# Two tiles at a time in the routed layers of a small fused transformer, with two smaller reorderings

## The reference, cut to what matters

```python
# layers 0 and 1, feed-forward: the best 2 of 8 experts for each token
logits = xn @ gate_w
top_logits, top_idx = jax.lax.top_k(logits, TOP_K)
h = jax.nn.gelu(jnp.einsum('td,edh->teh', xn, w1) + b1, approximate=False)   # 192 -> 768
y = jnp.einsum('teh,ehd->ted', h, w2) + b2                                   # 768 -> 192
# layer 2, attention: a local and a linear attention, mixed by a learned gate
# (sigmoid of a small network), then an output product
# layer 2, feed-forward: 8 sub-spaces of 16 features, the best 4 of 64 small experts in each
z = jnp.einsum('nd,sdr->nsr', xf, P)
scores = jnp.einsum('nsr,smr->nsm', z, C)
topv, topi = jax.lax.top_k(scores, K)
```

## Time and profile before

| what | value |
|---|---|
| median of 3 runs | 2105.56 us (2104.97 to 2110.13) |
| the profiled execution | 2113.81 us, of which the span of the trace is 2112.1 us |
| PE busy in the span | 1833.6 us, 87% |
| routed layers, tiles | about 291 to 451 us and 697 to 852 us of the span |
| fusion and gates | about 1031 to 1312 us |
| sub-experts | about 1313 to 1660 us |

### The profile page before, as it was taken

How to read it: one execution, slowest core, us unless ns; L and a number is a source line. 1 busy time by engine, 2 the same in 40 slices (tenths; PEclk the granted TensorE clock), 3 DMA queues, 4 the chain that set the end, 5 groups by cost and what they waited for, 6 DMA issues and landing times. The chain is left out here.

```text
span 2112.1 us, 38740 instructions
## 1 busy us (share of the span) xinstructions
PE 1833.6 (87%) x13908; PEld 1330.6 (63%) x14000; DVE 1218.9 (58%) x3641; ACT 837.8 (40%) x1667; POOL 379.5 (18%) x380
## 2 busy tenths in 40 slices
PE   5989969987885999788898775899999899979997
PEld 3678759966664799577655442333333588657886
DVE  1478842237998222488535544788888567792221
ACT  1145413324551111245335545667667355311111
POOL 1100112133311331431001101000000000123543
PEclk8999979998995899899898877999999999999999
DMA  5000345520004554102000104900000000304662
GB/s 200 1 1 0 115 136 179 187 57 18 12 0 142 168 187 156 30 19 85 0 1 17 48 29 128 291 24 1 1 1 1 24 1 0 133 13 132 188 179 64
DMA packets 83839, 156.75 MB, mean 74 GB/s; under 512 B 22390, under 2 KB 57942, under 8 KB 82806
## 3 DMA queue, kind: packets, MB, share of 16 engines
q1 hardware_dynamic: 63669, 134.71, 19.6%
q0 software_dynamic: 19552, 19.63, 3.9%
q10 hardware_dynamic: 480, 0.63, 0.1%
HBM read 125.04 MB, written 29.48 MB: 73 GB/s over the span
## 5 line engine op out<-in xcount | busy, mean ns | idle before, releaser
L2375 DVE TENSOR_TENSOR l2s_gated<-l2s_hidden,ps 128x408 f32<-128x408 f32 x512 | 262.8, 574 | 58.9 <-PE ps L2280 58.5
L2345 ACT ACTIVATE l2s_hidden<-ps,pack_l2f 128x816 f32<-128x816 f32 x256 | 227.0, 938 | 98.7 <-PE ps L2272 98.0
L129 PE MATMUL ps<-pack_const 128*128 128x512 bf16 x496 | 147.4, 432 | 40.6 <-PEq L163 13.7
L2280 PE MATMUL ps<-l2s_gs,l2s_spread 96*128 96x408 bf16 x512 | 150.5, 340 | 0.3 <-DVE l2s_gated L2375 0.3
L2272 PE MATMUL ps<-l2s_zs,l2s_up 128*128 128x408 bf16 x512 | 132.7, 341 | 15.7 <-DMA l2s_down<-in_sub_down 15.7
L1895 PE MATMUL ps<-l_down,l_hidden 128*128 x792 | 139.8, 326 | 0.0
L1895 PEld LDWEIGHTS ps<-l_down,l_hidden 128*128 128x128 f32 x792 | 127.3, 190 | 0.4
L129 PEld LDWEIGHTS ps<-pack_const 128*128 128x128 bf16 x588 | 59.4, 108 | 100.5 <-issue 62.4
L2290 PE MATMUL ps<-l2s_gated,l2s_down 128*32 128x408 f32 x1024 | 114.3, 518 | 4.0 <-DVE l2s_comb L2362 3.8
L2272 PEld LDWEIGHTS ps<-l2s_zs,l2s_up 128*128 128x128 bf16 x512 | 39.6, 97 | 120.5 <-ACT l2s_hidden L2345 82.2
L1854 POOL DMA_INDIRECT l_xt<-rows_in,l_tokens x66 | 63.1, 956 | 255.3 <-PE ps L1867 196.1
(11 more groups left out here) (468 smaller groups left out, 4007.4 us busy)
## 6 DMA issues: line engine op xcount, KB each, us to landing
l_up<-in_l_up SPq DMA_DIRECT2D x66, 576.0 KB, 3.8
l3c_wg<-in_l_gate SPq DMA_DIRECT2D x16, 576.0 KB, 4.9
l3c_wu<-in_l_up SPq DMA_DIRECT2D x16, 576.0 KB, 6.2
l3c_wd<-in_l_down SPq DMA_DIRECT2D x16, 576.0 KB, 3.9
slots_out<-l_y SPq DMA_DIRECT2D x66, 96.0 KB, 2.4
l_down<-in_l_down SPq DMA_DIRECT2D x8, 675.0 KB, 9.5
g_parts<-l2b_g_parts SPq DMA_DIRECT2D x12, 408.0 KB, 4.4
l_down<-in_l_down SPq DMA_DIRECT2D x8, 576.0 KB, 7.5
```

The lines of the kernel that those rows point to most:

```text
L129: pe.matmul(bank, halves[:, 0:128], halves[:, :], start=True, stop=True)
L2280: pe.matmul(gate_bank(n), spread[:, t % 8, :], gs[half][2 * r + odd][:, t // 8, pair, chunk(n % 2), :], start=True, stop=True).then_inc(ga ...
L2345: act.activation(hidden[:, p % kept, :, :], ps[:, 0, 2 * (p % 2):2 * (p % 2) + 2, 0:NG], ACT.Gelu_apprx_tanh, bias=w.at("b1")[:, s * MT + ...
L2375: dve.tensor_tensor(gated[:, n % ring, :], hidden[:, n // 2 % kept, n % 2, :], gate_bank(n), ALU.mult)\
```

## The change

Three things are changed.

1. Routed layers, on PE and DVE: tiles go in pairs. For tiles i and i + 1 PE makes the whole-row products of both, then the half-row products of both, then the transposes of tiles i + 2 and i + 3, then the second products of tiles i - 2 and i - 1. DVE follows the same order. `hidden` gets four buffers instead of two. The program of SP and that of POOL stay as they are.
2. Fusion and gates: on PE `lin_outputs(q)`, on DVE `lin_results(q)` and `fuse(q - 1)` now stand ahead of `step(at[2])` instead of behind it. ACT stays.
3. Sub-experts: the two parts of a block of weights have a semaphore each; the first product waits for the first part alone, the second product for the second part. SP issues the first part ahead of the block's gate parts.

```diff
-                step(at[2])
                 if q < G:
                     lin_outputs(q)
+                step(at[2])
...
-                step(at[2])
                 if q < G:
                     lin_results(q)
                 if 1 <= q <= G:
                     fuse(q - 1)
+                step(at[2])
                 step(at[3])
...
-        hidden = m.sb("hidden", [128, 2, FM, 128])
+        hidden = m.sb("hidden", [128, 4, FM, 128])
...
             transposes(0)
-            for i in range(TILES):
-                up_products(i)
-                if i + 1 < TILES:
-                    transposes(i + 1)
+            transposes(1)
+            for i in range(0, TILES, 2):
+                two = range(i, min(i + 2, TILES))
+                for n in two:
+                    whole_products(n)
+                for n in two:
+                    half_row_products(n)
+                for n in two:
+                    if n + 2 < TILES:
+                        transposes(n + 2)
                 if i:
-                    down_products(i - 1, expert_of(pe, i - 1))
-            down_products(TILES - 1, expert_of(pe, TILES - 1))
+                    for n in (i - 2, i - 1):
+                        down_products(n, expert_of(pe, n))
+            for n in two:
+                down_products(n, expert_of(pe, n))
...
-                if i >= 2:
-                    act.wait_ge(y_ps, i - 1)
+                if i >= 4:
+                    act.wait_ge(y_ps, i - 3)
...
             rows_turned(0)
+            rows_turned(1)
-            for i in range(TILES):
-                if i + 1 < TILES:
-                    rows_turned(i + 1)
+            for i in range(0, TILES, 2):
+                two = range(i, min(i + 2, TILES))
+                for n in two:
+                    if n + 2 < TILES:
+                        rows_turned(n + 2)
                 if i:
-                    result(i - 1)
-            result(TILES - 1)
+                    for n in (i - 2, i - 1):
+                        result(n)
+            for n in two:
+                result(n)
...
-                        pe.wait_ge(weights_loaded[k], 32)
+                        pe.wait_ge(up_loaded[k], 16)
...
+                    if not half and t == 0 and pair == 0 and at % 2 == 0:
+                        pe.wait_ge(down_loaded[2 * r + odd], 16)
```

More of the change, by code:

```diff
@@ L1868, in transposes, with whole_products @@
                 last.then_inc(xtT_ps, 1)
-            def up_products(i):
+            def whole_products(i):
                 pe.wait_ge(xtT_ready, i + 1)
@@ L1879, in up_products, with half_row_products @@
                                   xtT[:, i % 2, 0, :], start=(t == 0), stop=False, skip_group_check=True)
+            def half_row_products(i):
                 for t in range(3):
@@ L1894, in down_products @@
                 for t in range(FM):
-                    last = pe.matmul(y_bank(i), hidden[:, i % 2, t, :], wd[:, t * D:(t + 1) * D],
+                    last = pe.matmul(y_bank(i), hidden[:, i % 4, t, :], wd[:, t * D:(t + 1) * D],
                                      start=(t == 0), stop=(t == FM - 1))
@@ L1973, in _ @@
                             n = 3 * half + t
-                            last = act.activation(hidden[:, i % 2, n, :], hid_bank(i, half)[:, t * 128:(t + 1) * 128],
+                            last = act.activation(hidden[:, i % 4, n, :], hid_bank(i, half)[:, t * 128:(t + 1) * 128],
                                                   func, bias=b1[:, n:n + 1])
                     else:
-                        last = act.activation(hidden[:, i % 2, 3 * half:3 * half + 3, :].rearrange("p t n -> p (t n)"),
+                        last = act.activation(hidden[:, i % 4, 3 * half:3 * half + 3, :].rearrange("p t n -> p (t n)"),
                                               hid_bank(i, half), func)
@@ L2198, in sub_experts @@
         comb_ps, comb_ready, comb_added = m.sem("comb_ps"), m.sem("comb_ready"), m.sem("comb_added")
-        weights_loaded = [m.sem(f"weights_loaded{k}") for k in range(4)]
+        up_loaded, down_loaded = ([m.sem(f"{name}_loaded{k}") for k in range(4)] for name in ("up", "down"))
         parts_loaded = [[m.sem(f"parts_loaded{half}{k}") for k in range(4)] for half in range(2)]
@@ L2230, in _, with up_weights, down_weights @@
         def _(sp):
-            def weights(k):
+            def up_weights(k):
                 first = 4 * (k // 2) + k % 2
                 sp.dma_start(up_parts[k][:, :, :], g["up_pairs"][first:first + 3:2, :, :].rearrange("s k n -> k s n"))\
-                  .then_inc(weights_loaded[k], 16)
+                  .then_inc(up_loaded[k], 16)
+            def down_weights(k):
+                first = 4 * (k // 2) + k % 2
                 sp.dma_start(down[k][:, :, :, :].rearrange("p s t r -> p s (t r)"),
                              dram["sub_down"].rearrange("p (s n) -> p s n", s=NS)[:, first:first + 3:2, :])\
-                  .then_inc(weights_loaded[k], 16)
+                  .then_inc(down_loaded[k], 16)
             def parts(half, k):
@@ L2244, in parts @@
                   .then_inc(parts_loaded[half][k], 16)
-                if half or k:
-                    gate_parts(sp, half, k)
             sp.dma_start(spread_raw, dram["sub_spread"]).then_inc(spread_loaded, 16)
@@ L2252, in _ @@
                     if not half:
-                        weights(k)
+                        up_weights(k)
+                    if half or k:
+                        gate_parts(sp, half, k)
+                    if not half:
+                        down_weights(k)
                     if not half and k == 2:
```

## The result

The changed kernel takes 2194.34 us in the median (2190.86 to 2198.7) against 2107.85 us for the kernel before in the same series: ratio 1.0401, 95% interval 1.0371 to 1.0431. That is 86 us slower, where 60 were forecast; 2194 lies in the range given (2125 to 2202), near its upper end.

The account below looks back on a forecast made before the run. PE was taken to bound most stages, a chain through PE, ACT and DVE the fusion. Pairing -11, pauses +62, clock +22, fusion -12, sub-experts -1 give +60 on 2105.6: 2166 us, range 2125 to 2202.

Parts of the forecast that it names:

- The pauses: Routed layers: PE waits 2.2 us for weights ahead of odd tiles 5 to 31, 28 times, 62 us.
- The chain: Routed layers, after second products end at E: store E + 0.59, load E + 1.72, weights landed E + 5.5.
- rival 2: Routed layers: every pause costs clock, 2188 us, or loads also land half a microsecond later, 2202; chance 0.12.
- The clock: Routed layers: every second pause brings a stretch at half clock, 14 x 1.6 = 22 us lost.
- Rival 1: Routed layers: the clock holds through the pauses, 2144 us; chance 0.18.
- What pairing saves: Routed layers: 0.34 us for going into half-row products and out, paid once per two tiles, saves 11 us.
- The fusion: Fusion: the three PE pauses before the fused transposes go, 12 us saved, bounds 0 and 16.
- The sub-experts: Sub-experts: the first product no longer waits for the second part of the weights, 1 us saved, between 0 and 3.
- The sum: Whole kernel: -11 + 62 + 22 - 12 - 1 = +60 us, giving 2166 us for the median.
- the forecast's own range: Whole kernel: 2145 to 2190 us around the predicted 2166, with chance 0.50.
- rival 3: Routed layers: the pauses don't come, the store doesn't hold up the load or slack hides it; 2082 us; chance 0.13.

## Why the prediction was right, and where its sizes were off

**The pauses** came where they were forecast, ahead of each odd tile from 5 to 31, for the reason forecast: the load stands behind a store, and the store's result was moved behind the transposes. Moving the load was enough to undo them. The term was mis-sized: 62 us forecast, 75.5 measured, 2.7 us each instead of 2.2. The chain went the same way, most links a little longer. The second products end at 372.76 + 12 x 0.163 = 374.71; the store is issued at +0.72 (forecast 0.59), the load at +1.80 (1.72), and PE starts again at +5.92 (5.5), that is 4.1 us after the load's issue instead of 3.8. The loads now land more slowly, which the old median could not show:

```profile
DMA to landing us min/median/max: 3.5/4.5/7.5
```

against 3.8 before. That figure mixes both kinds: from tile 5 on the odd tiles' loads land in 4.1 us in the median, the even ones, which go out while the odd one is still under way, in 4.8. Only the odd ones' 0.3 us counts for the pauses. This was named under rival 2, with half a microsecond. The forecast's other figure, 3.35 us by the Trainium skill ("DMA: Bandwidth & Descriptors", section "Anatomy of one DMA"), is an estimate from a fit that the page gives for DMAs issued by GpSimd, and SP issues these; it was too low here.

**The clock.** 22 us forecast for every second pause, 31.1 measured. The step that was mis-sized is the share of pauses, which was a guess between none and all: one of two was taken, and the trace's record of the granted clock has a stretch at 0.50 behind 19 of the 28, 11 in layer 0 and 8 in layer 1. Each lasts 3.4 us and so costs 1.7, which makes 32 us. Rival 1, the clock that holds, is out: idle times of 2.1 to 3.2 us, once in 11 to 14 us, were enough to lose the full clock again and again, while others of 1.8 to 2.8 us went by without it. The Trainium skill ("TensorE: Matmul & The Clock Gate", section "HAM oscillation") has only longer idle gaps as harmful; the measurement decides. The length of the pause alone doesn't tell which outcome comes. Behind the pause of 2.46 us shown above the clock stayed at 1.00, behind the next one, of 2.45 us, it was 0.50:

```profile
392.04 2.07 PE L1878 MATMUL ps<-l_xtT,l_up 128*128 128x128 f32 x12 [2.45 <-issue]
393.00:396.40 3.40, 3.40 (x28) 3.17 (x28) 0.00 (x0) 0.51 (x2) 0.00 (x0) 0.50 0.06 26
```

What a slow stretch costs is seen on the half-row products of two pairs in succession, 2.86 us at the low level and 1.54 at the high one:

```profile
369.25:372.11 2.86, 2.86 (x25) 2.64 (x24) 0.00 (x0) 1.01 (x4) 0.00 (x0) 0.50 0.00 2
382.14:383.68 1.54, 1.54 (x25) 1.42 (x25) 0.00 (x0) 0.40 (x2) 0.00 (x0) 1.00 0.15 56
```

**What pairing saves**: 11 us forecast, 11.9 measured with the pauses gone. In the steady part two tiles took 9.05 us and a pair takes 8.71, the forecast's 0.34; the rest lies in the layers' starts.

**The fusion**: 12 us forecast, 13.4 in the profile, which alone is good to some 5 us, and 14 (8 to 18) in the timed runs of that part alone. For q = 2 the forecast had DVE's scores of the next step 11.5 us after the end of `gates`. In the changed kernel `gates` end at 1212.95 and the scores start here:

```profile
1211.94 1.01 DVE L1535 TENSOR_TENSOR rows_z<-ps,pack_l2a 102x384 f32<-102x384 f32 x2
1217.27 0.86 PE L1243 MATMUL ps<-pack_const,rows_z 102*96 102x102 f32 x8
1222.26 0.89 ACT L1392 ACTIVATE pack_l0f<-ps 96x408 f32<-96x408 f32 x2
1223.89 1.11 DVE L1579 MAX8 l2b_best<-x 102x8 f32<-102x64 f32 x8 [1.51 <-ACT x L1414]
```

That is 10.9 us, against 15.4 before. PE's transposes are early, at 1217.27, and their results lie until ACT copies them at 1222.26, behind its part of the step, as forecast. A little of the wait moved from L1243, where 11.6 us are gone, to L1305, which waited 5.5 us for ACT before and waits 7.4 now, three times each.

**The sub-experts**: 1 forecast, 1.0 in the profile; no run could tell it from nothing.

**The sum**: +60 forecast, +80 in the profile. The difference is 13 us of pauses and 9 us of clock, less 2 in the other terms. 2194 lies past the forecast's own range, which ended at 2190; the whole range held because rival 2 reached to 2202, and both things that rival 2 names came true in part: more pauses than one of two cost clock, and the odd tiles' loads land 0.3 us later. Nothing of rival 3 is in the profile. That the clock's term came within 9 us owes something to luck, since two rows with opposite outcomes were all it was taken from.

## What to carry to other kernels

When work is reordered on the engine that decides, write down for each queue what stands in front of every DMA issue. Here no line of SP was changed in the routed layers, and the odd tiles' loads came 2.7 us too late since a store in front of them waits for a result that had moved. Short pauses of a full TensorE cost more than their length: here 75 us of waiting brought 31 us of lost clock with it, and filling products in the pause are worth that much where the wait can't be removed. Grouping half-row products pays 0.3 to 0.4 us for each change of kind that it saves, but only once nothing new is waited for.

## What the runs showed of the hardware that was not expected

- The same 576 KB load lands in 4.5 us in the median where the loads go out in twos with a store between them, and in 3.8 where they go out evenly, though fewer bytes flow in the mean (133 against 172 to 179 GB/s). Where two go out 1.1 us apart with nothing between them, the first lands in 3.7 us and the second in 6.2.
- The time at the low clock fell almost wholly on work: of the changed kernel's 28 pauses only one, at 312 us, has low clock in it, 0.4 us. A pause and the slow stretch behind it add up, they don't overlap.
